# A four-layer transformer on one core: the fourth attention transposes two units' bytes per DMA and adds two overwritten matmuls ahead of each unit's products; the third layer's squared-relu feed-forward works in f32

## The reference

```
q(w) = sign * scale per group of 64 weights of a row:
       wb = bf16(w); scale = max(mean|wb|, 1e-8); clip(round(wb / scale), -1, 1) * scale
h    = relu(n @ q(W_fc).T) ** 2            # 1024 hidden features
h    = h * rsqrt(mean(h * h) + eps)
x   += h @ q(W_proj).T
```

## Time and profile before

| | us |
|---|---|
| median of 3 runs | 1208.64 (1208.03 to 1210.03) |
| profiled execution, its own time | 1204.26 |
| its span | 1202.5 |
| L2 feed-forward, first to last instruction | 560.0 to 657.3 |
| L3 attention, first to last exponential | 729.8 to 931.3 |

### The profile page before, as it was taken

One profiled execution on the slowest core, in us unless ns is written; L12 is line 12 of the kernel. 1 busy time (PEld: TensorE's weight loads), 2 busy tenths in 40 slices (PEclk: granted clock), 3 DMA queues, 4 the chain that ended last, 5 costly groups with the idle time before them and its releaser, 6 DMA issues. The chain is left out here.

```text
span 1202.5 us, 16226 instructions
## 1 busy us (share of the span) xinstructions
PE 937.2 (78%) x5648; PEld 530.0 (44%) x5648; DVE 657.8 (55%) x1205; ACT 566.2 (47%) x844; POOL 249.0 (21%) x389
## 2 busy tenths in 40 slices
PE   5688888996983487994367637677777589999998
PEld 3244446663771344342136422222223456666665
DVE  4577735444357754225796737788889431111224
ACT  3166662222226655786263146788788222222211
POOL 3010100000000022001241105666667014000013
PEclk9599998997996799996598956655555679999999
DMA  3512201003110047621000756999999402111112
GB/s 127 131 32 74 80 16 35 1 1 115 66 52 1 1 147 169 145 73 44 0 1 1 282 173 142 188 186 175 180 180 186 116 32 88 35 44 45 31 38 89
DMA packets 179922, 105.85 MB, mean 88 GB/s; under 512 B 141253, under 2 KB 168079, under 8 KB 178063
## 3 DMA queue, kind: packets, MB, share of 16 engines
q1 hardware_dynamic: 174994, 97.61, 34.7%
q0 software_dynamic: 1536, 4.20, 1.1%
q10 hardware_dynamic: 3312, 3.02, 0.7%
HBM read 57.66 MB, written 16.38 MB: 62 GB/s over the span
## 5 line engine op out<-in xcount | busy, mean ns | idle before, releaser
L2272 ACT ACTIVATE sb_l_E<-PS,sb_l_NB,sb_L3SQS 128x1024 int16<-128x1024 f32 x128 | 154.0, 1203 | 42.6 <-POOL sb_l_NB L2231 40.5
L2281 DVE TENSOR_REDUCE sb_l_NM<-PS 128x1 f32<-128x1024 f32 x128 | 154.3, 1221 | 32.7 <-PE PS L2250 30.5
L2250 PE MATMUL PS<-sb_l_K,sb_l_Q 128*128 128x512 bf16 x256 | 123.6, 585 | 18.6 <-ACT sb_l_E L2272 17.0
L682 DVE TENSOR_REDUCE sb_negmax<-PS 128x2 f32<-128x512 f32 x128 | 84.1, 690 | 31.9 <-PE PS L532 31.7
L1387 ACT ACTIVATE sb_hidden<-PS 128x512 f32<-128x512 f32 x39 | 23.3, 598 | 164.2 <-PE PS L1341 164.2
L2222 POOL CAST sb_l_EB<-sb_l_E 128x1024 bf16<-128x1024 int16 x96 | 99.4, 1036 | 5.8
L2260 PEld LDWEIGHTS PS<-sb_L3VI,sb_l_ET 128*128 128x128 bf16 x1024 | 42.8, 107 | 130.9 <-DMA sb_l_ET<-sb_l_EB 121.6
L1422 DVE TENSOR_TENSOR sb_hidden<-sb_hidden,PS 128x512 f32<-128x512 f32 x39 | 26.8, 688 | 124.8 <-ACT sb_hidden L1387 124.8
L668 ACT ACTIVATE sb_E<-PS 128x1024 f32<-128x1024 f32 x64 | 65.5, 1023 | 42.5 <-PE PS L595 42.4
L1341 PE MATMUL PS<-sb_L3w,sb_block_xT 128*128 x184 | 82.8, 592 | 0.0
L2260 PE MATMUL PS<-sb_L3VI,sb_l_ET 128*128 128x16 bf16 x1024 | 49.6, 177 | 39.7 <-DMA sb_l_ET<-sb_l_EB 37.5
(11 more groups left out here) (355 smaller groups left out, 1821.8 us busy)
## 6 DMA issues: line engine op xcount, KB each, us to landing
sb_Q<-q SPq DMA_DIRECT2D x48, 192.0 KB
sb_L3w<-L3w SPq DMA_DIRECT2D x16, 512.0 KB, 8.9
sb_K<-k SPq DMA_DIRECT2D x24, 192.0 KB
sb_W2E<-L3w SPq DMA_DIRECT2D x8, 512.0 KB, 9.2
q<-sb_q_parts SPq DMA_DIRECT2D x12, 256.0 KB, 4.0
xs<-zero_row SPq DMA_DIRECT2D x1, 2944.0 KB, 47.3
sb_block_x<-xs SPq DMA_DIRECT2D x23, 128.0 KB, 2.2
ys<-sb_block_y ACTq DMA_DIRECT2D x23, 128.0 KB, 2.4
```

Source lines behind the costliest of these rows:

```text
L682: dve.tensor_reduce(NM[:, g, 2 * b:2 * b + 2, j:j + 1], core.bank(shared_bank(("max", m))).rearrange("p (u k) -> p u k", k=SEQ), axis=AX.X ...
L2250: ins = pe.matmul(core.bank(2 * (n % SRING) + half), Q[:, h % RING, t * P:(t + 1) * P], K[:, h % RING, half * HALF:(half + 1) * HALF], sta ...
L2272: act.activation(E[:, n % ERING, :], S(n), ACT.Exp, bias=NB[:, n:n + 1], scale=scale_of(h, t), accum_out=ZS[:, n:n + 1]).then_inc(exped, 1)
L2281: dve.tensor_reduce(NM[:, n:n + 1], S(n), axis=AX.X, op=ALU.max, negate=True).then_inc(maxed, 1)
```

## The change

**L3 attention.** ACT writes the exponential as one byte (uint8) per element, interleaved: the even unit of a pair to the even bytes, the odd one to the odd bytes of a tile of 128 x 1024 x 2 bytes. SP transposes that tile as 128 x 1024 elements of 16 bits: 64 DMAs instead of 128, each of as many bytes as before, issued once both exponentials are there. The cast to bf16 now comes behind the transpose and reads every second byte: POOL does it in 7 of 8 units, DVE in 1 of 8, six units behind the bias. The products come eight units behind. Ahead of them PE does two matmuls of 384 columns (`KEEP`) into the columns 128 to 511 of the PSUM bank whose columns 0 to 127 take the products; nothing reads their result.

**L2 feed-forward.** Its first block is gone. The weights are loaded untransposed, quantised during the 64 steps of the L2 attention (DVE in 26 pieces of 512 elements, two ahead of a copy L993, in the pairs of steps 7 to 13 and 18 to 24; POOL in eight operations of 2048 elements), transposed by two DMAs and widened to f32. The second block works in f32: 2 matmuls up per unit and 1 down per tile and chunk, no splits, and DVE adds the tiles 0 to 3 before the tiles 4 to 7 are complete.

```diff
@@ attention_l2 (POOL; DVE's pieces are two reductions and two comparisons per quarter of 512)
+                for i in range(2):
+                    sp.wait_ge(weighted, i + 1)
+                    sp.dma_start_transpose(QWT.rearrange("p (b n) -> p b n", n=P), QW).then_inc(w_turned, 16)
...
+                def cast_weights(i):
...
+                    pool.tensor_copy(WB, ffn_weights[i].rearrange("p a b -> p (a b)")).then_inc(cast, 1)
+                def sign_weights(i):
+                    pool.wait_ge(below, 4 * (i + 1))
+                    pool.tensor_tensor(ABOVE, ABOVE, BELOW, ALU.subtract).then_inc(signed, 1)
...
+                def weight_signs(i):
+                    pool.wait_ge(signed, i + 1)
+                    pool.tensor_tensor(by_group(QW), by_group(ABOVE), SC[:, :].unsqueeze(2).to_broadcast([P, 32, GROUP]),
+                                       ALU.mult).then_inc(weighted, 1)
+                def widen(i):
+                    pool.wait_ge(w_turned, 16 * (i + 1))
+                    pool.tensor_copy(ffn_weights[i].rearrange("p a b -> p (a b)"), QWT)
                 for g in range(GROUPS):
+                    if g == 1:
+                        cast_weights(0)
+                    if g == 2:
+                        sign_weights(0)
+                        weight_signs(0)
+                        cast_weights(1)
+                    if g == 4:
+                        widen(0)
+                    if g == 5:
+                        sign_weights(1)
+                        weight_signs(1)
+                    if g == 7:
+                        widen(1)
@@ ffn_relu2
                     for c in range(NC):
-                        for i in range(PARTS):
-                            ins = pe.matmul(core.bank(n % URING), Q1[:, c, k * P:(k + 1) * P],
-                                            XP[:, i, c, th * HALF:(th + 1) * HALF],
-                                            start=(m == 0), stop=(m == NC * PARTS - 1))
-                            m += 1
+                        ins = pe.matmul(core.bank(n % 2), up_weights[:, k, c, :],
+                                        core.XT[:, c, th * HALF:(th + 1) * HALF], start=(c == 0), stop=(c == NC - 1))
...
-                for n in range(HC + 4):
+                for n in range(HC + 2):
                     go_up(n)
-                pe.wait_ge(p3, HC)
+                pe.wait_ge(squared, HC)
                 for j in range(4):
                     for k in range(HC):
-                        go_down(j, k)
-                    go_up(HC + 4 + j)
-                pe.wait_ge(relued, NU)
+                        ins = go_down(j, k)
+                    ins.then_inc(down, 1)
+                    go_up(HC + 2 + j)
+                for n in range(HC + 6, NU):
+                    go_up(n)
+                pe.wait_ge(relued, NU - 1)
+                pe.wait_ge(one_made, 1)
+                mean(0)
                 for k in range(HC):
-                    pe.wait_ge(p3, HC + k + 1)
+                    pe.wait_ge(squared, HC + k + 1)
                     for t in range(4, 8):
                         ins = go_down(t, k)
...
+                    if k == HC - 3:
+                        pe.wait_ge(relued, NU)
+                        mean(1)
@@ attention_l3
-    PER, BRING, TRING, LAG = 1, 6, 8, 7
+    CAST_LAG, LAG = 6, 8          # and KEEP = 2, TRING = 5, CRING = 4
-    by_pool = [u % 8 in (0, 1, 2, 4, 5, 6) for u in range(NU)]
+    by_pool = [u % 8 != 5 for u in range(NU)]
...
+                for m in range(NU // 2):
+                    sp.wait_ge(exped, 2 * m + 2)
                     if m >= TRING:
+                        wait_cast(sp, 2 * (m - TRING) + 1)
+                    sp.dma_start_transpose(EP[:, m % TRING].rearrange("p k q i -> p k (q i)").bitcast(U16),
+                                           E[:, m % ERING].rearrange("p k i -> p (k i)").bitcast(U16)
                                            ).then_inc(turned[m % TRING], 16)
...
             def cast(eng, u):
+                wait_turned(eng, u // 2)
+                if u >= CRING:
+                    eng.wait_ge(mixed, u - CRING + 1)
+                return eng.tensor_copy(ET[:, u % CRING], EP[:, u // 2 % TRING, :, :, u % 2])
...
-                        wait_turned(pe, u // PER)
...
+                        for i in range(KEEP):
+                            pe.matmul(core.PS[:, 6 + h % 2, P:4 * P], core.identb[:, :],
+                                      VI[:, 0:2, :].rearrange("p t d -> p (t d)")[:, 0:3 * P], start=True, stop=True)
+                        wait_cast(pe, u)
...
-                    act.activation(E[:, n % ERING, :], S(n), ACT.Exp, bias=NB[:, n:n + 1], scale=scale_of(h, t),
-                                   accum_out=ZS[:, n:n + 1]).then_inc(exped, 1)
+                    if n % 2 == 0 and n // 2 >= ERING:
+                        wait_turned(act, n // 2 - ERING)
+                    act.activation(E[:, n // 2 % ERING, :, n % 2], S(n), ACT.Exp, bias=NB[:, n:n + 1],
+                                   scale=scale_of(h, t), accum_out=ZS[:, n:n + 1]).then_inc(exped, 1)
```

More of the change, by code:

```diff
@@ L17 @@
 BF16 = mybir.dt.bfloat16
[L18 removed]
+U8, U16 = mybir.dt.uint8, mybir.dt.uint16
 U32 = mybir.dt.uint32
@@ L746, in attention_l2 @@
     NS = len(steps)
+    GROUP, LIMIT, QUARTER, FIRST_PAIR = 64, 0.5 + 2.0 ** -9, 512, (7, 18)
+    cast, reduced, scaled_w, above, below, signed, weighted, w_turned = (core.sem(n) for n in (
+        "cast", "reduced", "scaled_w", "above", "below", "signed", "weighted", "w_turned"))
     names = ("q_projected", "v_projected", "squared", "meaned", "logged", "inverted", "scaled", "high", "rest", "middle",
@@ L989, in _ @@
                     n = s // 2
+                    for i in range(2):
+                        for m in range(2 * (n - FIRST_PAIR[i]), 2 * (n - FIRST_PAIR[i]) + 2):
+                            if 0 <= m < 13:
+                                quantise_weights(i, m)
                     if b == 0 and g >= 2:
@@ L1832, in ffn_relu2 @@
     HC = HID // P
-    GROUP = 64
-    LIMIT = 0.5 + 2.0 ** -9
     EPS = float(np.finfo(np.float32).eps)
-    with ExitStack() as ctx:
[L1837 to L1897, removed]
@@ new lines, in ffn_relu2 @@
+    up_weights = W1.rearrange("p k (c n) -> p k c n", c=NC)
+    down_weights = W2.rearrange("p c (k n) -> p c k n", k=HC)
+    names = ("up", "relued", "squared", "quart", "pooled", "meaned", "eps_added", "rooted", "inverted", "down",
+             "one_made", "added")
+    (up, relued, squared, quart, pooled, meaned, eps_added, rooted, inverted, down,
+     one_made, added) = (core.sem(n) for n in names)
+    units = [(th, k) for th in range(2) for k in range(HC)]
+    NU = len(units)
+    down_bank = lambda t: core.PS[:, 3 + t // 2, (t % 2) * D:(t % 2 + 1) * D] if t < 4 else core.PS[
+        :, (2, 5, 6, 7)[t - 4], 0:D]
@@ L1905, in ffn_relu2 @@
         RS = core.sb(ctx, "rs", [P, NT], F32)
[L1906 to L1912, removed]
-        down_bank = lambda t: core.PS[:, 3 + t // 2, (t % 2) * D:(t % 2 + 1) * D] if t < 4 else core.PS[
-            :, (5, 6, 7, 1)[t - 4], 0:D]
         with nc.Block() as block:
@@ L1941, in _, with mean @@
+                def mean(th):
+                    pe.wait_ge(pooled, HC * (th + 1))
+                    for j in range(4):
+                        ins = pe.matmul(core.PS[:, th, j:j + 1], SUM[:, th, j * P:(j + 1) * P], ONE[:, :],
+                                        start=True, stop=True)
+                    ins.then_inc(meaned, 1)
+                for n in range(HC + 2):
                     go_up(n)
-                pe.wait_ge(p3, HC)
+                pe.wait_ge(squared, HC)
                 for j in range(4):
@@ L1972, in _, with root @@
             def _(act):
-                for n in range(NU + 2):
+                def root(th):
+                    T = slice(4 * th, 4 * th + 4)
+                    act.wait_ge(eps_added, th + 1)
+                    act.activation(RS[:, T], MS[:, T], ACT.Sqrt).then_inc(rooted, 1)
+                for n in range(NU + 1):
                     if n < NU:
@@ L2226, in _ @@
                 pool.memset(K[:, :, :].bitcast(F32), 0.0).then_inc(cleared, 1)
-                for n in range(NU + 2):
+                for n in range(NU + CAST_LAG):
                     if n < NU:
```

184 lines of the change are left out of this document (90 added, 94 removed).

## The result

The changed kernel takes **1155.4 us** (median of 4 runs, 1153.9 to 1158.6) against 1209.0 for the kernel before on the same chip: ratio 0.956, 95% interval 0.954 to 0.958. 1158 us was predicted. Its profiled execution took 1153.91 us, span 1152.1, against 1204.26 and 1202.5.

The account below looks back on a forecast made before the run. It took transposing DMAs to pace the L3 attention, POOL's order next, and the L2 feed-forward's preparation to lie on the path. -33.9 + 1 - 17.6 = -50.5 took 1204.26 to 1153.8; plus 4.4, 1158 us (1138 to 1184).

Parts of the forecast that it names:

- Steps 1 to 3: L2 feed-forward: first block's 30.4 us go, f32 block takes 61.0, tail 2.0; end 623.4 against 657.3, -33.9 us.
- Step 4: L2 attention: the quantising moved into it mostly fits beside the existing work; +1 us (0 to 6).
- rival E: L2 attention: the moved quantising costs the end of its range, 6 us, giving 1163 us; chance 0.05.
- Step 5: L3 attention: 64 transposes for 128, DMA share about 0.6, landing 3.3 us; the queue no longer the pace.
- Step 6: L3 attention, POOL's order: POOL's byte cast 1.04 us, POOL unit 1.45, DVE unit about 1.30, average 1.43.
- rival C: L3 attention: byte cast dear on POOL; at 1.2 us 1176 us, at 2.03 us 1269 us; chance 0.11.
- Step 7: L3 attention, extra matmuls: PE 1.90 us a unit at low clock, about 1.05 at full; low briefly, then high, +2 us.
- rivals A and B: L3 attention: PE clock swings (A, 1188 us, chance 0.14) or stays low for good (B, 1216 us, chance 0.03).
- Step 8: L3 attention's sum: -18.7 us for its pace, start +2, loads +1, end -1.9; together -17.6 us.
- start and loads: L3 attention: +2 us for a low clock in the first units, +1 us for loads beside the transposes.
- Rival D: L3 attention: POOL doesn't bind, ACT sets 1.30 us a unit, -17 us, giving 1141 us; chance 0.17.

## Why the prediction was right

**Steps 1 to 3, the feed-forward.** Predicted 623.4 for its end, 622.04 measured. From the first product to the last PE took 60.1 us (559.81 to 619.94) where 61.0 stood. The tail behind it is 2.1 us, for 2.0, and the run with late adds shows what it saves: 4.05 us from end to end, 4.5 behind the last product. Not in the sum: the stage after it gives 1.5 us more; its first 32 matmuls, behind a PE that stood for a shorter time, take 1.6 us less.

**Step 4** was put at +1 us; it is 0.5 to 0.6, by the run without it. The end of the range, rival E, is out.

**Step 5** held: share 0.60, landing 3.1 us in the median, and with the number of DMAs doubled the old pace returns. That the DMA queue itself was the pace, and not SP's issuing, isn't shown.

**Step 6** has the one term of weight that was mis-sized, the DVE unit. POOL's byte cast is 1.040 us, and POOL's unit 1.453: as predicted, which ends rival C. The DVE unit was put at 1.30 and measured 1.69. The step took DVE's cast out of DVE's slack, as if it could start at will; in fact it started under a cast of POOL's, waited that out, and held up POOL's bias. The eight units were to cost 7 x 1.45 + 1.30 = 11.45 us and cost 11.86: over 16 groups, 6.6 us too little. Placed later it costs less than POOL's own, as the step wanted: 11.27. The trace of before showed most of it: its DVE unit takes 1.42 us, not 1.30. The other 0.27 is the price of the bytes: 0.55 us left after POOL's end instead of 0.29, and 0.68 us in quiet where int16 has its smallest at 0.417. The group's mean of 0.597, on which the 1.30 rested, mixes both kinds of start. In the earlier trace rows DVE's 6.15 us beside POOL's 4.05 is a case of such waiting too (2.15 us of it after POOL's end, against 2.29 alone), and was charged in step 4 and forgotten here.

The Trainium skill has the rule, in SBUF — State Buffer, section "SBUF: two separate sides": of a GpSimd operation and a VectorE one in a fast mode, the one that starts first holds the shared ports for its whole instruction, and the other waits. The trace agrees both ways: 1.38 us where POOL started first, of them 0.55 after POOL's end (0.13 less than the 0.68 in quiet, as 0.29 is against 0.417 for int16), and 0.64 instead of 0.27 for POOL's bias where DVE started first. The Trainium skill's page VectorE: DVE Perf Modes (What auto-detection actually checks) was read too narrowly in the prediction. By it a cast of every second byte loses the packed reads alone; the mode that spreads one source over two ports asks for source and destination in SBUF and for outermost dimensions that are even or equal, which both have here. So the page has about half of a one-per-cycle pass, an estimate of 0.61 us from the 1.22, not 1.22. The 0.68 in quiet agrees; the 1.324 of the list only looked like a lost fast mode.

**Step 7.** The clock behaved as forecast, high for all of 710 to 880. But the argument that the clock decides was wrong: without the matmuls PE took no 1.90 us a unit, since those 0.66 us were the matmuls' own. At the low clock a unit without them is 1.24 us, inside POOL's 1.45, and the run without them kept the pace. So rivals A and B were dangers that only the added matmuls could have brought, and in the kernel as changed the matmuls bought nothing. The +2 us of the start didn't come: the first units run ahead at 1.19 us apart.

**Step 8.** -17.6 predicted for the attention. Measured: -12.9 to the last exponential (-15.7 predicted, with start and loads), and from its end to the end of the last products 6.3 us after 7.8, -1.5 (-1.9 predicted). The DVE unit was 6.6 us too cheap; start and loads, +3, didn't come, since the pace as measured gives 127 x 1.482 = 188.2 and 187.4 was measured. The two errors partly cancel.

In all -50.5 was predicted of the profiled execution and -50.35 measured. That closeness is luck: the feed-forward, with step 4 and the stage behind it, gave 3.8 us more than the -32.9 they were put at, the attention and all behind it 3.9 less than its -17.6. The median came out under the 1158 because it lies 1.5 us above the profiled execution after the change, where 4.4 was kept.

**Rival D** (POOL doesn't bind) is out in the kernel as changed. All casts on POOL give 1.449 a unit, POOL's own order. Even with the later cast seven units in eight stand at POOL's 1.45; the eighth, at 1.10, waits for DVE's maximum, and the exponentials alone could follow at 1.19.

## What to carry to other kernels

When work is handed from a busy engine to one with slack, place it in time before counting it: on engines that lock each other out, the same cast cost 0.70 us or 1.32 in the mean by where it stood in the order, and the wrong place was worse than no hand-over. A mean in the list of groups holds such waiting: ask for the smallest and the largest, and look at one instance beside its neighbours, before taking it for the operation's price. And ask of anything that raises a clock which wait ends on that engine: here two matmuls lifted it from 0.50 to 1.00 for no time at all, until another edit put the scores on the path.

## What the runs showed of the hardware

A cast of every second byte to bf16, 1024 elements a partition, costs POOL 1.040 us, as much as the packed int16 one, and DVE 0.68 us when POOL is quiet (0.42 for packed int16). With one transposing DMA of 256 KB a unit, and the loads of later heads beside them, a unit takes 1.58 us, and 1.60 where 64 of the 128 carry a copy that nobody reads. To issue one takes SP 1.23 us at least, in the full stage and in the changed one alike. An exponential with a sum, 1.206 us and 0.191 for the read of the accumulator, can follow its predecessor after 1.19 us.
